# Score stages in sixteen small tiles, condition rows from TensorE, and a set-up reordered, in an attention and mixture kernel

## The reference, cut to what matters

```python
sc = einsum('bhnid,bhnjd->bhnij', Qb, Kw) / sqrt(D)
sc = where(mask, sc, -inf); p = softmax(sc)
```

## Time and profile before

| what | value |
|---|---|
| median of 3 runs | 1327.85 us |
| profiled execution, its own time | 1326.44 us |
| its span | 1324.6 us |
| TensorE busy | 1181.0 us, 89% |
| VectorE busy | 906.8 us, 68% |
| ScalarE busy | 711.2 us, 54% |
| GpSimd busy | 214.9 us, 16% |
| mean granted TensorE clock | 0.961 of full |

### The profile page before, as it was taken

How to read it: one execution, slowest core, us unless ns; L and a number is a source line. 1 busy time by engine, 2 the same in 40 slices (tenths; PEclk the granted TensorE clock), 3 DMA queues, 4 the chain that set the end, 5 groups by cost and what they waited for, 6 DMA issues and landing times.

```text
span 1324.6 us, 34251 instructions
## 1 busy us (share of the span) xinstructions
PE 1181.0 (89%) x13940; PEld 826.7 (62%) x13940; DVE 906.8 (68%) x3547; ACT 711.2 (54%) x1460; POOL 214.9 (16%) x176
## 2 busy tenths in 40 slices
PE   3867778989999999999999999999999989888776
PEld 1444445656666676767777676767676766666555
DVE  4557877877777797779777877697877784342412
ACT  0256676655567664575557655756575463333221
POOL 0301103012030220213021301122011220101101
PEclk8888898989999999999999999999999999999888
DMA  9210010001001010100000000000000000000000
GB/s 317 73 64 13 18 29 26 9 26 38 2 16 47 10 41 11 42 10 31 21 26 18 18 26 22 22 3 29 2 30 15 18 15 18 10 10 18 2 9 8
DMA packets 26974, 38.55 MB, mean 29 GB/s; under 512 B 3472, under 2 KB 21264, under 8 KB 26816
## 3 DMA queue, kind: packets, MB, share of 16 engines
q1 hardware_dynamic: 25472, 34.79, 8.3%
q10 hardware_dynamic: 1344, 1.57, 0.4%
HBM read 31.67 MB, written 4.29 MB: 27 GB/s over the span
## 4 chain that ended last, share of the span: by engine, by line
PE 68%; DVE 15%; ACT 12%; issue 3%; DMA 1%; POOL 0%; SPq 0%; DVEq 0%; POOLq 0%; ACTq 0%
PE psg L434 42%; PE psq L434 14%; PE pso L434 6%; PE psg L437 6%; ACT PQ L1337 6%; DVE TU L893 2%; DVE nm L896 1%; ACT QK L1337 1%; DVE ST L890 1%; DMA QK<-in_w_ada 1%; ACT M L1337 1%; ACT L1337 1%; DVE smf L890 1%; ACT JA L1348 1%; ACT OT L1340 1%
## 5 line engine op out<-in xcount | busy, mean ns | idle before, releaser
L1337 ACT ACTIVATE PQ<-psq 128x1280 f32<-128x1280 f32 (+2 forms) x144 | 215.5, 1496 | 102.2 <-PE psq L434 101.4
L1686 POOL TENSOR_TENSOR R<-R,rhoT 128x512 f32<-128x512 f32 x64 | 82.7, 1292 | 522.6 <-ACT R L1337 522.1
L434 PE MATMUL psg<-zT,WiT 128*128 128x256 f32 x512 | 126.0, 390 | 1.3 <-DVE R L893 1.3
L434 PE MATMUL pso<-PQ,Vg 128*32 128x256 f32 (+2 forms) x2048 | 116.8, 347 | 8.6 <-ACT PQ L1337 8.6
L434 PE MATMUL psq<-QK 32*128 32x128 f32 (+4 forms) x3328 | 123.2, 304 | 0.0
L434 PE MATMUL psg<-WoT,R 128*128 128x256 f32 x512 | 113.6, 379 | 0.0
L896 DVE TENSOR_REDUCE nm<-psq 128x16 f32<-128x2048 f32 (+1 forms) x48 | 92.8, 1933 | 26.1 <-PE psq L434 26.0
L434 PEld LDWEIGHTS psg<-zT,WiT 128*128 128x128 f32 x512 | 94.5, 194 | 16.5 <-issue 2.7
L434 PEld LDWEIGHTS psq<-QK 32*128 32x128 f32 (+1 forms) x3328 | 94.2, 166 | 16.4 <-issue 7.7
L434 PEld LDWEIGHTS psg<-WoT,R 128*128 128x128 f32 x512 | 95.9, 190 | 13.0 <-issue 0.5
L434 PE MATMUL psg<-wqkv,M 128*128 128x512 f32 (+1 forms) x256 | 97.8, 511 | 0.8 <-DVE ST L890 0.8
(11 more groups left out here) (223 smaller groups left out, 2360.3 us busy)
## 6 DMA issues: line engine op xcount, KB each, us to landing
bcA<-ada_rows SPq DMA_DIRECT2D x16, 384.0 KB, 3.4
bcB<-ada_rows SPq DMA_DIRECT2D x16, 384.0 KB, 3.4
X<-in_x SPq DMA_DIRECT2D x16, 256.0 KB, 4.3
XR<-in_x SPq DMA_DIRECT2D x16, 256.0 KB, 2.8
out<-XR SPq DMA_DIRECT2D x16, 256.0 KB, 2.2
QK<-NMT SPq DMA_DIRECT2D x128, 3.0 KB
WiT<-in_WiT SPq DMA_DIRECT2D x1, 1024.0 KB, 5.0
WoT<-in_WoT SPq DMA_DIRECT2D x1, 1024.0 KB, 7.6
```

Of the source, the lines that this page charges most:

```text
L434: return e.matmul(o, lhsT, rhs, start=start, stop=stop, skip_group_check=True)
L1337: return e.activation(o, i, func, **kw)
L1686: e.tensor_tensor(R4, R4, rhoT[:, :].unsqueeze(1).broadcast_to([128, 2, 256]), ALU.mult).then_inc(*pool_moe.mark(b, f"r{f}"))
```

## The change

- In `maxi` steps "a" and "b", in `lat` and in `loc`, the score matmuls use the same 16 tiles of 32x32 as the masks: 64, 64, 16 and 32 float32 matmuls a stage in place of 16, 32, 8 and 8. Step "l" stays.
- `ada` replaces TensorE's `setup`: first three rows of batch 0 over all 128 partitions ("bc": the condition column broadcast as weights), which VectorE adds to the bias straight into `bcA[0]`, then the 16-partition rows in three steps. The scratch rows are written in three parts under two signals; batch 0's `bcA` is not read back.
- `w_ada` is loaded in four parts, the first 768 columns first; its second half lies in `R2`, so `w1T1` and `w21` wait for nothing. The loads have a new order. `WG` is made in `psq` in eight steps (four matmuls each) instead of two in `psg`; the loads' waits stand at their first use.
- `prep` unit 0 holds batch 0 alone; then [1, 2], [3].
- `ORDER` is a new table for all engines.

```diff
--- before.py
+++ after.py
...
-        "**n*qqqq**nhqhqqaqaaaan*aaaooohhoqaqqaaqaaaanaooohhoqaqqaaqaaaaaNooFFohhoaaaaaaaaooppppppomommnmNqqqFFql",
...
+        "AA*AAn*qqqq*******hhn*qqqqa*anaaaaaaooohhqqqqaoaaaaaaanooohhqqqqaoaaaaaaNaooFFohhoaaaaaaaaooppppppomomnN",
+        "mmqqqqFFlnlkkhqhqqqkkkkkkawwNaawwaawaaFFapwoopppppwmeeohmhoemmaapappaaeeaaaleoolkekknNkqqqqFFonkkokkehhe",
...
-        wada = ST1.rearrange("p j n -> p (j n)"), QK2[0].rearrange("p e n -> p (e n)")[:, 0:1536]
+        wada = ST1.rearrange("p j n -> p (j n)"), R2.rearrange("p f n -> p (f n)")[:, 0:1536]
...
-        quad = Banks([psq], dve_late.at(0, "ada3"))
-        po, pg = Banks([pso]), Banks(psg)
+        quad = Banks([psq], dve_ada.at(0, "a3"))
+        po, pg = Banks([pso], dve_ada.at(0, "a5")), Banks(psg)
         pq, pslot = Banks([0, 1]), {}
 
 
 
-        units = [([0, 1], []), ([2, 3], []), ([], [0])]
+        units = [([0], []), ([1, 2], []), ([3], []), ([], [0])]
...
+            def ada(_):
+
+                yield
                 w.wait_ge(*loads["cond"])
                 for c in range(2):
-                    w.wait_ge(*loads[f"wada{c}"])
-                for j in range(3):
+                    w.wait_ge(*loads[f"wada{c}0"])
+                for j, n in ((0, 512), (1, 256)):
                     for c in range(2):
-                        last = mm(psq[0:16, j, :], condT[:, c, :], wada[c][:, 512 * j:512 * j + 512], c == 0, c == 1)
-                    last.then_inc(*pe_setup.mark(0, f"ada{j}"))
-                w.wait_ge(*pool_setup.at(0, "ones"))
-                for k in ("wqkv", "wo"):
-                    w.wait_ge(*loads[k])
+                        last = mm(psq[:, j, 0:n], condT[:, c, 0:1].broadcast_to([128, 128]), wada[c][:, 512 * j:512 * j + n],
+                                  c == 0, c == 1)
+                last.then_inc(*pe_ada.mark(0, "bc"))
+                for j, o in enumerate((psq[0:16, 2, :], psq[0:16, 3, :], pso[0:16, :])):
+                    yield
+                    if j:
+                        for c in range(2):
+                            w.wait_ge(*loads[f"wada{c}1"])
+                    for c in range(2):
+                        last = mm(o, condT[:, c, :], wada[c][:, 512 * j:512 * j + 512], c == 0, c == 1)
+                    last.then_inc(*pe_ada.mark(0, f"r{j}"))
 
             def late(_):
             def late(_):
                 for ic in range(2):
-                    yield
-                    bank = take(pg, ("W", ic), act_late.at(0, f"W{ic}"))
-                    for k in ("w1T0", "w1T1", "w20", "w21"):
-                        w.wait_ge(*loads[k])
                     for f in range(8):
+                        if f % 2 == 0:
+                            yield
+                        if f == 0:
+                            w.wait_ge(*dve_ada.at(0, "c2"))
+                        w.wait_ge(*loads[f"w1T{f // 4}"])
+                        w.wait_ge(*loads[f"w2{f // 4}"])
                         v = wx[f // 4][:, f % 4, :]
-                        last = mm(bank[:, :], v[:, 128 * ic:128 * ic + 128], v, f == 0, f == 7)
+                        last = mm(psq[:, ic, :], v[:, 128 * ic:128 * ic + 128], v, f == 0, f == 7)
                     last.then_inc(*pe_late.mark(0, f"W{ic}"))
                 yield
                 bank = take(pg, ("b1w",), act_late.at(0, "b1x"))
...
                     mm(psq[o, i, :].rearrange("p (r n) -> p r n", r=4), unit(r),
                        MQ[r, 96 - 32 * j:224 - 32 * j].unsqueeze(1).broadcast_to([32, 4, 128]), True, False)
                 for ek in range(4):
                     ee, k = ek // 2, ek % 2
-                    for i in range(4):
-                        r = slice(32 * i, 32 * i + 32)
-                        last = mm(psq[:, i, 128 * ek:128 * ek + 128], qk[r, ee, 256 * k:256 * k + 128],
+                    for i, j, r, o in tiles():
+                        q0 = 256 * k + 32 * j
+                        last = mm(psq[o, i, 128 * ek:128 * ek + 128], qk[r, ee, q0:q0 + 32],
                                   qk[r, ee, 768 + 256 * k:896 + 256 * k], False, True)
                 last.then_inc(*pe_max.mark(b, "a"))
...
-                    for half in range(2):
-                        for i in range(4):
-                            r = slice(32 * i, 32 * i + 32)
-                            q0, k0 = 256 * k + 128 + 64 * half, 768 + 256 * k + 64 + 64 * half
-                            last = mm(psq[64 * half:64 * half + 64, i, 128 * ek:128 * ek + 128], qk[r, ee, q0:q0 + 64],
-                                      qk[r, ee, k0:k0 + 128], False, True)
+                    for i, j, r, o in tiles():
+                        q0, k0 = 256 * k + 128 + 32 * j, 832 + 256 * k + 64 * (j // 2)
+                        last = mm(psq[o, i, 128 * ek:128 * ek + 128], qk[r, ee, q0:q0 + 32], qk[r, ee, k0:k0 + 128],
+                                  False, True)
...
                     mm(psq[o, i, 0:256], unit(r), MLT[r, m:m + 256], True, False)
-                for ee in range(2):
-                    for i in range(4):
-                        r = slice(32 * i, 32 * i + 32)
-                        last = mm(psq[64 * ee:64 * ee + 64, i, 0:256], qk[r, ee, 1280:1344], qk[r, ee, 512:768], False, True)
+                for i, j, r, o in tiles():
+                    ee, n = j // 2, 1280 + 32 * (j % 2)
+                    last = mm(psq[o, i, 0:256], qk[r, ee, n:n + 32], qk[r, ee, 512:768], False, True)
...
-                    for o, ks_, qs in ((slice(0, 192), 0, slice(0, 192)), (slice(192, 320), 128, slice(128, 256))):
-                        for i in range(4):
-                            r = slice(32 * i, 32 * i + 32)
-                            k0, q0 = 768 + 256 * k + ks_, 256 * k + qs.start
-                            last = mm(psq[:, i, o], qk[r, ee, k0:k0 + 128], qk[r, ee, q0:256 * k + qs.stop], False, True)
+                    for s, n, first in ((0, 192, 0), (192, 128, 128)):
+                        for i, j, r, o in tiles():
+                            k0, q0 = 768 + 256 * k + first + 32 * j, 256 * k + first
+                            last = mm(psq[o, i, s:s + n], qk[r, ee, k0:k0 + 32], qk[r, ee, q0:q0 + n], False, True)
...
+                for k, i in enumerate((psq[:, 0, 0:256], psq[:, 0, 256:512], psq[:, 1, 0:256])):
+                    stt(bcA[0][:, k, :], i, float(k == 1), bada[0][:, 256 * k:256 * k + 256], ALU.add,
+                        ALU.add)().then_inc(*s.mark(0, f"c{k}"))
...
-                load(e, "bqkv", bqkv[:, :], A["bqkv"].partition_broadcast(128))
-                load(e, "bo", bo[:, :], A["b_o"].partition_broadcast(128))
+                load(e, "cond", condT[:, :, :], A["condT"].rearrange("(c p) b -> p c b", p=128))
+                load(e, "bada0", bada[0], A["b_ada"][0:768].partition_broadcast(128))
                 load(e, "w1T0", wx[0][:, :, 0:256], chunks("w1T")[:, 0:4])
                 load(e, "w20", wx[0][:, :, 256:512], chunks("w2")[:, 0:4])
+                load(e, "bqkv", bqkv[:, :], A["bqkv"].partition_broadcast(128))
+                load(e, "bada1", bada[1], A["b_ada"][768:1536].partition_broadcast(16))
+                load(e, "bo", bo[:, :], A["b_o"].partition_broadcast(128))
 
...
-                load(e, "cond", condT[:, :, :], A["condT"].rearrange("(c p) b -> p c b", p=128))
                 for c in range(2):
-                    load(e, f"wada{c}", wada[c], chunks("w_ada")[:, c])
-                load(e, "bada0", badaR[0], A["b_ada"][0:768].partition_broadcast(16))
-                load(e, "bada1", badaR[1], A["b_ada"][768:1536].partition_broadcast(16))
+                    load(e, f"wada{c}0", wada[c][:, 0:768], chunks("w_ada")[:, c, 0:768])
+                load(e, "ident", ident0, A["ident"])
+                load(e, "wqkv", wqkv[:, :, :], chunks("wqkv"))
+                for c in range(2):
+                    load(e, f"wada{c}1", wada[c][:, 768:1536], chunks("w_ada")[:, c, 768:1536])
                 for _ in x_load(1):
                     pass
-                load(e, "ident", ident0, A["ident"])
-                load(e, "wqkv", wqkv[:, :, :], chunks("wqkv"))
-                load(e, "hsel", hsel[:, :], A["hsel"])
-                load(e, "wo", wo[:, :, :], chunks("w_o"))
-                for b in range(2, 4):
-                    for _ in x_load(b):
-                        pass
-                load(e, "b1c", b1c, A["b1c"])
-
-            def late(_):
-
-                chunks = lambda k: A[k].rearrange("(c p) n -> p c n", p=128)
-                yield
-                w.wait_ge(*pe_setup.at(0, "ada2"))
                 load(e, "w1T1", wx[1][:, :, 0:256], chunks("w1T")[:, 4:8])
                 load(e, "w21", wx[1][:, :, 256:512], chunks("w2")[:, 4:8])
-                yield
-                w.wait_ge(*dve_late.at(0, "one1"))
-                for j in range(3):
-                    e.dma_start(scratch[:, 512 * j:512 * j + 512], adaR[j]).then_inc(loads["ada"][0], 16)
```

(46 more changed lines are left out.)

211 lines of the change are left out of this document (116 added, 95 removed).

## The result

The changed kernel takes 1341.01 us in the median of four runs (1340.06 to 1346.54), the kernel before 1327.01 beside it (1326.06 to 1328.44): ratio 1.0113, 95% interval 1.0083 to 1.0143, 14 us slower. The forecast was 1350, its own range 1338 to 1362: the time lies 3 us inside its lower end. The profiled execution's span is 1338.4 us.

What follows compares the result with a forecast made beforehand. TensorE was taken to bound the kernel between 300 and 1100 us, so work added there moves the end by its length. Profiled 1326.4 + 44 (score stages) - 20 (set-up) + 0 (table, smaller edits) = 1350 us, range 1338 to 1362.

Steps and rivals of the forecast that it cites:

- Part 1: Score stages on TensorE: 16 tiles wait for results under a limit of 64 unfinished instructions, +44 us.
- rival B: Score stages: the limit counts instructions not yet started, so feeding four per 17 ns binds; -5 us, 1301 us; chance 0.12.
- Part 2: Set-up before batch 0's `heads`: it starts at 43 instead of 64.86 us; -20 us, bounds 0 and -26.
- the 2 us of work to be done later: Set-up: 2 us allowed for work now in the idle 26 us (`b1b`, `w2sq`, the 16-partition rows).
- Rival C: Whole kernel: the instruction limit holds and the set-up gain is lost in the ramp; 1370 us; chance 0.12.
- Part 3: Order table, waits at first use and smaller edits: 0 us, the table's bounds -12 and +10.
- Rival D: Limit holds, but the new table hides a third of 44, above all in the tail, and gives -8; 1328 us; chance 0.12.

Runs made afterwards that it cites:

- first experiment: The changed kernel with the four score stages back in their shapes of before: 1289.95 us, run again 1288.17 us; ratio to the kernel before 0.971, then 0.970.
- second experiment: The kernel before with only the four score stages of the change in 16 tiles: 1376.09 us, ratio 1.036.
- fifth experiment: The kernel before, own set-up and score shapes, with only the new order table and `prep` grouping: 1313.57 us, ratio 0.989.

## Why the prediction was right, and where it was off

**Part 1, the score stages: right by mechanism; of the size, the stages were right and the stops missing.** Each stage came within 0.05 us of its forecast, 2.59 us a batch or 41 us in all, where 44 were said. The first two experiments give +51 and +48 us for the tiles. Beyond the 41 of the stages, the stops named "issue" are 4.8 and 7.3 us; they were not in the sum, and some 5 of the 51 stay unassigned.

That finished results free the places, 64 of them, can be counted in the trace of the change. In the step at 179.92, with the instructions numbered in program order (load, pass, load, pass for each tile) and the passes told apart by their durations, nine loads in a row, at 180.73 to 180.89, start 0.030 to 0.032 us after the result of the matmul 65 instructions before them, and over the 32 such steps no load of the rounds so counted starts earlier than 0.030 us after it. A load doesn't wait for its own tile instead: the first of the nine starts at 180.73, before its tile's last matmul has its result at 180.75. (The three instants of the "b" step in the prediction, 440.02, 440.10 and 440.07, are each some 0.01 us early by the trace; the 0.03 us from result to load holds.) The rounds agree, 0.41 us for 128 columns and 0.32 for 64: by rival B a round would be 0.27 for either. The Trainium skill's "TensorE: Matmul & The Clock Gate", section "Measured speedup vs the span model", has about 4 ns for each further tile. The masks agree (one lasts 0.385 us, sixteen together 0.44); for a round of scores, two passes of 0.109 and 15 further tiles make an estimate of 0.28, and the trace's 0.41 decides against it here.

**Part 2, the set-up: -20 said, -25 measured** (fifth experiment to the first). First matmul at 8.54 (8 to 10 said), `heads` at 47.14 (43). I had `qkv` from 20 to 25; it runs from 23.79 to 30, and the 17 us of products behind it are as said. Its start is late by TensorE's own order: the last operation on its input ends at 17.88 on GpSimd (19 said), but TensorE makes two of the three steps of 16-partition rows from 18.04 first, so the transpose is at 21.58, and four matmuls of `WG` from 22.07 stand between it and `qkv`. I had counted those rows in the 2 us of work to be done later, not ahead of the transpose. The forecast put the gain on the earlier start in general; the runs put it on the condition rows, without which 24 of the 25.4 us are gone, and some 10 of it is TensorE's busy time at a higher clock, which the sum didn't have. Rival C, the gain lost in the ramp, is refuted, though the 12 us at the first `maxi` look like it.

**Part 3, the table: the step that failed.** I took 0 between -12 and +10; it is -15.7, outside my bounds. The low bound was too tight: the tail gave back 20 of its 42 us of idle time, and I had allowed 12. The granted clock of the tail rose with it, from 0.92 to 0.98. Rival D named the gain in the tail, but also that the table would hide part of the tiles' cost, and it hides none: +51 with the new table, +48 with the old.

**The sum** came out 9 us too high because -15.7 and -5 were missing on one side and +7 on the other. That the time lies in the range is in part luck: with the table as measured and the rest as forecast it would be 1334, under the range, and the tiles' 7 us brought it back. The measured parts, 1326 + 51 - 25 - 16 = 1336 against 1341, are no test of the account: they are steps along one chain of kernels and have to add up. The 5 us between come from using different runs of the same kernels (1289.95 and 1288.17 for the first experiment; 1326, 1327.01 and 1329.26 for the kernel before). The independent test is the second experiment, +48 for the tiles in the old surroundings.

## What to carry to other kernels

Equal tile shapes save a gap of about 0.1 us, but a float32 matmul in 16 tiles of 32x32 needs four times the instructions of a 128-wide weight, and short ones come to wait for results, and in long rows for the instructions themselves: count instructions for each column streamed before cutting a tile. Measure the parts of a change each by itself: here a part worth -41 us hid under one of +51, and the best kernel is the change without the tiles it was named after. In a ramp, look at the chain of the first batch and not at an engine's idle time: a row that goes through DRAM (11.6 us) and a filler among the steps of that chain (8.6 us at its transpose) both came back at the end in full or more, and both with a lower clock.

## What the hardware showed that I had not expected

**TensorE can run out of instructions.** The kernel before has no stop of a matmul with the releaser "issue", the change nine (4.8 us), its tiles alone 7.3 us, "a" and "b" wide again 0.5, "a" doubled 35.2 us in 21 stops, 32.8 of it in its scores. One in the changed kernel, and its instruction queue (packets, MB):

```profile
q8 instruction: 156, 2.56, 0.8%
...
222.22 0.41 PE L435 MATMUL psq<-QK 32*32 32x128 f32 x4 [0.90 <-issue]
```

TensorE has 27,880 instructions before, 39,672 in the change and 43,768 with "a" doubled, and this queue 109, 156 and 172 packets of 16 KB: it brings TensorE's program, some 255 instructions in each. The packets' times show what the stops wait for. All 40 stops of the four kernels that have them, from 0.2 to 2.4 us long, end 1.2 to 1.6 us after one of these packets has landed; the one above ends at 222.22, its packet at 220.88. In these kernels no two packets start less than 3.25 us apart, while the small tiles use 64 instructions in 0.41 us, a packet in 1.6. In the kernel before and in the first experiment, without stops, the nearest packets are 5.1 and 4.3 us apart.

So a long row of short instructions uses up what has been fetched. Where no score stage has more than 160 instructions, as before and in the first experiment, there are no stops; with "a" at 544 each of the 16 has its stop. What sets the 3.25 us was not tested, and no run changes the fetching by itself.
